# Splitting six groups of a CIN kernel's first layer instead of four, and moving one copy in the first chunk

## The reference, cut to what matters

```python
def _cin_layer(x0, xi, W):
    F0_, Fi, Fn = (x0.shape[1], xi.shape[1], W.shape[-1])
    Wr = W.reshape(F0_, Fi, Fn)
    return jnp.einsum('bid,bjd,ijn->bnd', x0, xi, Wr)
h = x
outs = []
for W in (W0, W1, W2):
    h = _cin_layer(x, h, W)
    outs.append(h)
res = jnp.concatenate(outs, axis=1)
return jnp.sum(res, axis=-1)
...
h = jnp.concatenate([z, dense_ctx], axis=1)
h = jnp.maximum(h @ W_top1 + b_top1, 0.0)
h = jnp.maximum(h @ W_top2 + b_top2, 0.0)
y = h @ W_top3
```

## Time and profile before

| | us |
|---|---|
| median of 3 runs | 1139.14 (1136.38 to 1140.77) |
| the profiled execution's own time | 1139.9 |
| its span, first to last instruction | 1138.1 |
| PE (TensorE matmul) busy | 1100.9 (97%) |
| DVE (VectorE) busy | 901.2 (79%) |
| POOL (GpSimd) busy | 913.9 (80%) |
| ACT (ScalarE) busy | 684.9 (60%) |

### The profile page before, as it was taken

One profiled execution on the slowest core, in us unless ns is written; L12 is line 12 of the kernel. 1 busy time (PEld: TensorE's weight loads), 2 busy tenths in 40 slices (PEclk: granted clock), 3 DMA queues, 4 the chain that ended last, 5 costly groups with the idle time before them and its releaser, 6 DMA issues.

```text
span 1138.1 us, 17464 instructions
## 1 busy us (share of the span) xinstructions
PE 1100.9 (97%) x4802; PEld 818.8 (72%) x4802; DVE 901.2 (79%) x2567; ACT 684.9 (60%) x2132; POOL 913.9 (80%) x848
## 2 busy tenths in 40 slices
PE   2898999999999999999999999999999999999999
PEld 2666677777778777777678777777777777777775
DVE  2788788988887788888887698989887588988750
ACT  3354666666664566666665466766665466666751
POOL 6778798989989598898889689898988769966740
PEclk8899899999999999999999999999999999999999
DMA  7573514252444425243251634315153621523000
GB/s 267 132 182 66 140 34 112 46 119 57 94 119 103 104 45 113 64 92 85 39 134 48 164 82 85 87 18 140 28 131 82 164 63 29 129 79 127 1 1 1
DMA packets 128100, 102.51 MB, mean 90 GB/s; under 512 B 77569, under 2 KB 87041, under 8 KB 127490
## 3 DMA queue, kind: packets, MB, share of 16 engines
q1 hardware_dynamic: 117714, 92.89, 33.0%
q0 software_dynamic: 8192, 2.11, 2.2%
q10 hardware_dynamic: 2096, 6.40, 1.4%
HBM read 97.16 MB, written 4.20 MB: 89 GB/s over the span
## 4 chain that ended last, share of the span: by engine, by line
PE 80%; POOL 12%; DMA 3%; issue 2%; DVE 1%; ACT 1%; SPq 0%; POOLq 0%; ACTq 0%; DVEq 0%
PE tps L870 19%; PE tps L872 18%; PE tps L871 18%; PE acc L828 8%; POOL ysum_sb L450 5%; PE side L897 5%; POOL rows_sb L429 4%; PE side L884 3%; PE acc L812 2%; PE acc L817 2%; PE acc L813 2%; PE acc L823 1%; PE side L892 1%; PE tps L964 1%; POOL ysum_sb L447 1%
## 5 line engine op out<-in xcount | busy, mean ns | idle before, releaser
L688 ACT ACTIVATE y_sb<-tps,xcol_sb 128x128 f32<-128x128 f32 x1792 | 511.5, 375 | 365.2 <-PE tps L872 325.4
L571 DVE SCALAR_TENSOR_TENSOR parts_sb<-tps,xcol_sb,parts_sb 128x128 f32<-128x128 f32 x2176 | 604.9, 341 | 152.1 <-PE tps L872 150.4
L450 POOL TENSOR_TENSOR ysum_sb<-ysum_sb,y_sb 128x512 f32<-128x512 f32 x319 | 421.0, 1320 | 72.7 <-ACT y_sb L688 50.0
L870 PE MATMUL tps<-w_hi_sb,h_hi_sb 128*128 128x512 f32 x1024 | 464.8, 454 | 6.2 <-ACT y_sb L688 4.6
L871 PE MATMUL tps<-w_lo_sb,h_hi_sb 128*128 128x512 f32 x1024 | 405.9, 396 | 0.0
L872 PE MATMUL tps<-w_hi_sb,h_lo_sb 128*128 128x512 f32 x1024 | 405.9, 396 | 0.0
L429 POOL DMA_INDIRECT rows_sb<-tables,rows_now_sb x240 | 255.4, 1064 | 61.4 <-issue 25.5
L870 PEld LDWEIGHTS tps<-w_hi_sb,h_hi_sb 128*128 128x128 f32 x1024 | 193.4, 189 | 97.2 <-issue 25.7
L871 PEld LDWEIGHTS tps<-w_lo_sb,h_hi_sb 128*128 128x128 f32 x1024 | 193.8, 189 | 65.6 <-issue 28.8
L872 PEld LDWEIGHTS tps<-w_hi_sb,h_lo_sb 128*128 128x128 f32 x1024 | 193.4, 189 | 46.6
L519 DVE TENSOR_TENSOR prod_sb<-roll_sb,xx_ps 128x1024 f32<-128x1024 f32 (+1 forms) x136 | 155.9, 1146 | 14.1 <-DMA roll_sb<-x_halves 12.7
(11 more groups left out here) (72 smaller groups left out, 607.6 us busy)
## 6 DMA issues: line engine op xcount, KB each, us to landing
roll_sb<-x_scratch SPq DMA_DIRECT2D x240, 256.0 KB, 4.2
w_sb<-w_rows SPq DMA_DIRECT2D x40, 256.0 KB, 4.2
gsum_sb<-w_rows ACTq DMA_DIRECT2D x8, 512.0 KB, 8.9
roll_sb<-x_halves SPq DMA_DIRECT2D x32, 128.0 KB, 2.9
rows_sb<-tables,rows_now_sb POOLq DMA_INDIRECT x240
x_scratch<-rows_sb SPq DMA_DIRECT2D x30, 128.0 KB, 4.1
xx_sb<-x_scratch SPq DMA_DIRECT2D x15, 256.0 KB
roll_sb<-x_scratch SPq DMA_DIRECT2D x30, 64.0 KB, 1.9
```

The source lines that it names most:

```text
L450: pool.tensor_tensor(ysum[:], ysum[:], y[:, bank], ALU.add).then_inc(y_step, 1)
L571: dve.scalar_tensor_tensor(part, bank, scale, part, ALU.mult, ALU.add).then_inc(d_done, 1)
L688: done = act.activation(y[:, bank, u * NF:(u + 1) * NF], tps[:, p % RING, u * NF:(u + 1) * NF], ACT.Copy, scale=xcol[:, (q + 1) % 2, s, i: ...
L870: pe.matmul(bank, h1_hi[:, par, cols], w1_hi[:, of], start=True, stop=False, skip_group_check=True)
```

## The change

`SPLIT` becomes (1, 2, 3, 5, 6, 7), so groups 2 and 6 are split as well and only 0 and 4 stay raw (`RAW` follows from it). `hi` gets two buffers, used in turn, and the rounding waits for the split group before the previous one. In the first chunk alone ScalarE's copy of `xx` for the third chunk moves from place 56 to place 63.

```diff
-SPLIT = (1, 3, 5, 7)
+SPLIT = (1, 2, 3, 5, 6, 7)
...
-FIRST_STORE_AT, FIRST_XX_LOAD_AT = 48, 50
+FIRST_STORE_AT, FIRST_XX_LOAD_AT, FIRST_XX_COPY_AT = 48, 50, PLACES - 1
...
-        hi = sb("hi", [P, 2, CH], F32R)
+        hi = sb("hi", [P, 2, 2, CH], F32R)
...
-                dve.tensor_tensor(lo[:, slot], prod[:, slot], hi[:].bitcast(F32), ALU.subtract).then_inc(lo_ready, 1)
+                dve.tensor_tensor(lo[:, slot], prod[:, slot], hi[:, SPLIT.index(g) % 2].bitcast(F32), ALU.subtract).then_inc(lo_ready, 1)
...
-                if e > 0:
-                    act.wait_ge(prod_used, t * GROUPS + (SPLIT[e - 1] + 1))
+
+                if e > 1:
+                    act.wait_ge(prod_used, t * GROUPS + (SPLIT[e - 2] + 1))
                 else:
-                    act.wait_ge(prod_used, t * GROUPS + (SPLIT[-1] + 1 - GROUPS))
+                    act.wait_ge(prod_used, t * GROUPS + (SPLIT[e - 2] + 1 - GROUPS))
...
-                act.activation(hi[:], prod[:, ring_place(q, g, 2)], ACT.Copy).then_inc(hi_ready, 1)
+                act.activation(hi[:, e % 2], prod[:, ring_place(q, g, 2)], ACT.Copy).then_inc(hi_ready, 1)
...
-                    if p == XX_COPY_AT and gathers(t):
+                    if p == (FIRST_XX_COPY_AT if q < 0 else XX_COPY_AT) and gathers(t):
                         copy_xx(t + 2)
...
-                        pe.matmul(acc[:], w0_hi[:, 2 * e + i, :], hi[:, i, :], start=False, stop=False, skip_group_check=True)
-                        pe.matmul(acc[:], w0_lo[:, 2 * e + i, :], hi[:, i, :], start=False, stop=False, skip_group_check=True)
+                        pe.matmul(acc[:], w0_hi[:, 2 * e + i, :], hi[:, e % 2, i, :], start=False, stop=False, skip_group_check=True)
+                        pe.matmul(acc[:], w0_lo[:, 2 * e + i, :], hi[:, e % 2, i, :], start=False, stop=False, skip_group_check=True)
```

## The result

The changed kernel took **1159.06 us** (1158.6 to 1159.18, 3 runs) against 1139.14 before: the ratio is 1.0186, with a 95% interval of 1.017 to 1.0202. It is slower by about 20 us. The forecast was 1145.3 in a range of 1128 to 1152: the side was right, the size was three times too small, and the time lies outside the range.

A forecast was written before the change was run, and what follows sets the result against it. TensorE sets the pace with GpSimd right behind; 0.5 + 4.8 + 4.8 - 2.0 - 0.7 + 0.4 - 1.6 = +6.2 us on 1139.9 makes 1146.1, less 0.8 for the median: 1145.3, range 1128 to 1152.

The forecast's parts named there:

- ring: The four banks ahead of TensorE swallow VectorE's 0.42 us wait of chunk 7, once in each of four groups: -1.6 us.
- GpSimd's pace: Regular chunks, place 48: with `h2t` slack used up, a chunk changes by GpSimd's +1.6 us, not TensorE's -0.68; chance 0.50.
- The second meets smaller gaps; I cost it at nothing: VectorE's added subtraction at place 40, 1.48 us, costs nothing since about 7.5 us of a chunk are free there.
- Rival 3: VectorE a second bound: place 40's subtraction brings half of 1.5 us to TensorE in 11 chunks, +8, 1153; chance 0.13.
- The hold of about 0.8 us per subtraction: GpSimd beside VectorE's added subtractions: each holds it 0.8 us, between 0 and 1.21, so 1.6 us more per chunk.
- The prediction's own sign for that: TensorE waiting for VectorE with no `h2t` wait near would show VectorE as second bound and the forecast wrong.
- Rival 2: Half the hold: added subtractions cost GpSimd 0.4 us each, between its instructions; -2.6 us, 1136.5; chance 0.20.
- rival 1: TensorE keeps the pace: `y`'s buffers and the ring absorb GpSimd's lag at place 48; 1124.6 us, faster; chance 0.17.
- The copy: ScalarE's copy of `xx` in chunk 0, moved to place 63, removes idling and low clock: 7.3 us, bounds 3 to 7.3.
- The copy's gain is eaten by chunk 3: Chunks 0 to 3: GpSimd -4.7 in chunk 0, +6.4 for eight subtractions, 1.23 us to spare; together +0.5.
- The W2 chunks: Chunks 4, 8 and 12, where GpSimd catches up: TensorE's gain of 0.68 us each, -2.0 in all.
- TensorE's saving: Two more split groups save TensorE 2 x 0.34 = 0.68 us per chunk, 10.2 us over 15 chunks.

## Why the prediction was wrong

By its own groups of chunks, the changed kernel's profiled run against that of before:

| | forecast | measured |
|---|---|---|
| chunks 0 to 3 | +0.5 | +5.3 (chunk 0 -2.9, the others +8.2) |
| chunks 5 to 7 | +4.8 | +5.75 |
| chunks 9 to 11 | +4.8 | +7.5 |
| chunks 4, 8, 12 | -2.0 | +0.8 (-0.4, +2.9, -1.7) |
| chunk 13 | +0.4 | +0.7 |
| chunk 14 | -0.7 | -0.65 |
| ring | -1.6 | none seen |
| sum | +6.2 | +19.3 |

That chunks 5 to 7 come near the forecast is in part luck: the 2.5 us of chunk 5 are VectorE's stretch, and only chunks 6 and 7 stand at GpSimd's pace, with 0.7 and 2.6.

**The step that failed** is "The second meets smaller gaps; I cost it at nothing", for the subtraction at place 40. Two things were wrong with it. It took the 7.5 us of a chunk that VectorE has free as cover, though the free time must lie in the same 22 places (32 to 54); an average over a chunk says nothing of that stretch. And it priced a subtraction by its median of 1.48 us. On the stretch that fills up, the three subtractions take 2.63, 2.94 and 1.79, and places 32 to 54 take 2.6 us more than before. The kernel with group 6 alone has regular chunks of 64.95 us, and the changed kernel with group 6's operand in PSUM has 62.8 where GpSimd does not pace it: this one instruction per chunk is worth 2 us and more.

**Rival 3** named this mechanism and its place, with 0.13. It gave half of 1.5 us in each of 11 chunks; the six settled chunks pay 2.5 us over the 62.63 of before. And it was added to my sum, where it takes its place: with VectorE the bound, GpSimd's pace costs nothing in most chunks (5.5 us to spare in chunk 3, where 1.23 had been).

**GpSimd's pace** was right as a mechanism and wrong in rank. The hold of about 0.8 us per subtraction stands: GpSimd's instructions that overlap a subtraction are longer than the median of their line by 0.73 us per subtraction in the mean, both before and after. One reading of the earlier trace rows was wrong without touching the size: the two did not end when the other let go. The subtraction of 396.60 ended at 398.57 and the gather at 399.40; each was long by what it waited for an instruction ahead of it, the subtraction for GpSimd's add and the gather for the subtraction. GpSimd paces chunk 7 of the changed kernel, where the wait for `h2t` grew from 0.42 to 2.78 us, and with one group less it paces more of them. "Chunks 2, 3, 6, 7, 10 and 11 should take 64 to 66 us" came out for three of six, with chunks 3 and 7 just above (66.2) and chunk 6 below (63.3), and mostly for the other reason. The prediction's own sign for that, TensorE waiting for VectorE with no `h2t` wait near, is what the rows of chunk 2 show.

**Rival 2**, half the hold, and **rival 1**, TensorE keeps the pace, needed GpSimd to pay less. Rival 1's time is near what the changed kernel takes once the holding is gone: 1120.75 measured, 1124.6 worked out.

**The copy** was right by itself: 7.3 worked out, 6.8 measured. (It moved behind four banks, those of places 56, 58, 60 and 62, and not three.) "The copy's gain is eaten by chunk 3" gave the right total, as undoing the move showed, and the wrong place: the gain was gone within chunk 0. Two added subtractions were to cost chunk 0 3.0 us; the changed kernel's chunk 0 is 6.3 us longer than with the copy alone (75.78 against 69.46), and 5.1 of it is holding, since with PSUM operands it takes 70.69.

**The W2 chunks** were to gain 0.68 each. Chunk 12 gained 1.7, as it lost a wait of 1.1 us for W2's rows that the kernel before had; chunk 8 lost 2.9, with a wait of 2.7 us for W2's rows. The prediction looked at GpSimd's path through `h2t` only and not at what its late gathers hold: a store, and behind it the loads.

**TensorE's saving** was over-sized: 0.68 us per chunk worked out, 0.46 measured. The part missing lies in places 0 to 32 around group 2. What takes it was not tried; the profiles show at place 26 a matmul that reaches ScalarE's copy too early (the copy ends at 200.49 and the matmul starts at 200.54, chunk 2 of the run with PSUM operands), and that place is 0.2 us longer than with four groups.

**Left open.** GpSimd hardly waits in the regular chunks of the changed kernel either (0.8 us at the most in one piece, around its gathers), and holds its 5.5 us of spare time from chunk to chunk. So the two engines move in step. That the holding is the cause is shown, by 38 us; which of the two would be the slower by itself under it was not separated. The two bounds are near each other: where GpSimd paces, a chunk takes from 64.2 us (chunks 3, 6 and 11 with group 6's operand in PSUM) to 66.2 (chunk 7 of the changed kernel), and where VectorE's stretch does, 65.1. So clearing that stretch alone wins its 2.5 us only while GpSimd has spare time.

## What to carry to other kernels

An instruction's cover must be looked for in the places around it, not in the engine's idle sum over a stage. Where an added instruction shares a resource with an engine that never rests, price it by the mean and the maximum that its like already shows, on both engines, and then expect it to be longer in a stretch where it meets no pause. Follow a late engine through every consumer: its sums, and also the transfers it feeds and whatever stands behind them in the same queue.

## What the runs showed of the hardware

A VectorE operation of 128x1024 with both inputs in SBUF takes 1.21 us at best and up to 3.04 beside a GpSimd that always works: it can lose against two of GpSimd's instructions in a row. With one input in PSUM, 90 of 90 took 1.207 to 1.222 us, and GpSimd's own instructions were shorter too. I had expected a loss of about one hold per instruction. The loss grows steeply with the number of such subtractions: 4 to 7 us of a run with 60, 38 with 90.

TensorE's idle time showed only 1.4 of the 2.5 us that a chunk lost: short delays between banks (0.53 us where 0.23 is usual) leave no gap, since the profile models a matmul's end and gives it some 0.4 us.
